# A transformer layer on one core: routed experts over token lists instead of over all tokens

## The reference

```python
h = take(weight, x)                                  # 8 x 1024 x 256
h = h + attn(layernorm(h)); h = h + ffn(layernorm(h))
# attn: L = 8 positions, N = 1024 sequences, 16 heads of 16; qkv = x @ qkv_proj.T + bias;
#       softmax(q k / 4) over the 8 positions of the same sequence; @ v; @ out_proj.T + out_bias
# ffn:  scores = sigmoid(flat @ Wg.T)                # T x 16
#       groups of 4 experts; the 2 groups with the largest sum of their top 2 stay; top 4 experts
#       topk_w = 2.5 * scores / sum(scores of the 4)
#       hid = relu(flat @ W1[e].T) ** 2              # 16 experts, 256 -> 128
#       out = sum over e of cw[t, e] * (hid @ W2[e].T)
#       shared = relu(flat @ Ws1.T) ** 2 @ Ws2.T     # 256 -> 256 -> 256
```

## Time and profile before

| | |
|---|---|
| median of three runs | 1466.54 us (1464.06 to 1471.74) |
| span of the profiled execution | 1464.6 us |
| PE, PE weight loads, DVE busy | 87%, 71%, 81% |
| ACT, POOL busy | 46%, 47% |
| DMA moved | 92.21 MB, mean 63 GB/s |

### The profile page before, as it was taken

How to read it: one execution, slowest core, us unless ns; L and a number is a source line. 1 busy time by engine, 2 the same in 40 slices (tenths; PEclk the granted TensorE clock), 3 DMA queues, 4 the chain that set the end, 5 groups by cost and what they waited for, 6 DMA issues and landing times.

```text
span 1464.6 us, 22940 instructions
## 1 busy us (share of the span) xinstructions
PE 1267.7 (87%) x7488; PEld 1033.1 (71%) x7488; DVE 1189.9 (81%) x1792; ACT 679.8 (46%) x1138; POOL 689.5 (47%) x753
## 2 busy tenths in 40 slices
PE   4458898889888899888989889898988989989898
PEld 2146767768677687767778677776867768677787
DVE  3868889697987969789797888969798797978854
ACT  2234444544444454444544444454553445445355
POOL 7744535365263635535464363536526363442600
PEclk9579999999999999999999999999999999999999
DMA  2302111111211112111111212112121111212122
GB/s 66 125 16 74 58 60 58 61 62 55 73 62 57 58 44 88 58 61 58 66 65 44 78 67 62 58 46 73 58 73 58 61 58 44 88 44 73 59 73 73
DMA packets 33748, 92.21 MB, mean 63 GB/s; under 512 B 4800, under 2 KB 13376, under 8 KB 33600
## 3 DMA queue, kind: packets, MB, share of 16 engines
q1 hardware_dynamic: 30528, 81.99, 16.7%
q0 software_dynamic: 3072, 8.39, 2.0%
HBM read 81.46 MB, written 8.91 MB: 62 GB/s over the span
## 4 chain that ended last, share of the span: by engine, by line
DVE 39%; PE 31%; issue 19%; POOL 5%; ACT 5%; DMA 1%; DVEq 1%; ACTq 0%; POOLq 0%; SPq 0%
PE psY L900 9%; PE psH L887 8%; DVE ring L684 7%; PE psB L927 5%; DVE p_sb L641 5%; DVE hid_lo L647 5%; PE psA L966 3%; DVE g_gt L723 2%; DVE ring L300 2%; PE psA L978 2%; DVE ring L302 2%; DVE ring L279 1%; DVE k_sb L666 1%; ACT hid_hi L510 1%; DVE stats L659 1%
## 5 line engine op out<-in xcount | busy, mean ns | idle before, releaser
L900 PE MATMUL psY<-w_hi,hid_hi 128*128 128x256 f32 x1152 | 339.0, 294 | 53.6 <-DVE hid_lo L647 50.3
L510 ACT CAST hid_hi<-p_sb 128x512 fp32r<-128x512 f32 x256 | 159.2, 622 | 388.8 <-DVE p_sb L641 379.5
L900 PE MATMUL psY<-w_lo,hid_hi 128*128 128x256 f32 x1152 | 330.5, 287 | 0.0
L900 PE MATMUL psY<-w_hi,hid_lo 128*128 128x256 f32 x1152 | 330.2, 287 | 0.0
L279 POOL TENSOR_TENSOR ring<-q_sb,k_sb 128x1024 f32<-128x1024 f32 x64 | 169.1, 2653 | 309.1 <-PE psA L940 205.2
L900 PEld LDWEIGHTS psY<-w_hi,hid_hi 128*128 128x128 f32 x1152 | 223.6, 194 | 107.4 <-DVE hid_lo L647 72.6
L647 DVE TENSOR_TENSOR hid_lo<-p_sb,hid_hi 128x512 fp32r<-128x512 f32 x256 | 214.6, 838 | 93.4 <-ACT hid_hi L510 73.7
L887 PE MATMUL psH<-xT_hi,w_hi 128*128 128x512 f32 x576 | 235.6, 409 | 10.9 <-issue 8.7
L641 DVE TENSOR_TENSOR p_sb<-r_sb,cwB 128x512 f32<-128x512 f32 x256 | 214.2, 837 | 34.1 <-ACT r_sb L499 27.2
L900 PEld LDWEIGHTS psY<-w_lo,hid_hi 128*128 128x128 f32 x1152 | 224.6, 195 | 9.8
L887 PE MATMUL psH<-xT_lo,w_hi 128*128 128x512 f32 x576 | 230.2, 400 | 0.0
(11 more groups left out here) (133 smaller groups left out, 2137.5 us busy)
## 6 DMA issues: line engine op xcount, KB each, us to landing
cwB<-cw_dram SPq DMA_DIRECT2D x128, 512.0 KB, 3.7
out<-h SPq DMA_DIRECT2D x32, 256.0 KB, 5.4
p_sb<-w_t SPq DMA_DIRECT2D x3, 512.0 KB
cwB<-w_t SPq DMA_DIRECT2D x3, 512.0 KB, 4.5
h<-w_t SPq DMA_DIRECT2D x2, 512.0 KB
xin<-table,idx_now POOLq DMA_INDIRECT x56
cwB<-wqkv_t SPq DMA_DIRECT2D x2, 384.0 KB, 3.2
cw_dram<-cwT SPq DMA_DIRECT2D x16, 32.0 KB, 1.6
```

The lines of the kernel that those rows point to most:

```text
L510: nc.scalar.copy(hid[0][:, e % 2, :], src[:, e % 2, :]).then_inc(hid_hi, 1)
L900: last = nc.tensor.matmul(psY[:, j // 2, (j % 2) * D:(j % 2 + 1) * D], hid[a][:, e % 2, j * P:(j + 1) * P], W2[b][:, e, :], start=(e == 0 ...
```

## The change

The kernel is rewritten in three phases, with no hardware loop; all steps are unrolled.

Phase 1 has 20 steps; step i does QKV of block i, scores and softmax of block i-1, values and output projection of block i-2, and of block i-3 the logits, the routing, the shared expert and the places of its rows. The sums over positions are now matmuls (`msum`, same form as the scores). DVE makes five of the eight products, POOL three. The values and the probabilities go to DRAM and come back in another layout (`values_io`, `probs_io`). The normalised row of a token, with its 16 weights and 16 destinations behind it (288 words), is scattered to each of the token's four experts' lists in DRAM by indirect DMA, 16 per block, the places being counted with a prefix matmul. The rows with the shared part go to `hd`.

Phase 2 runs 143 units of 256 list places. A table says for each unit its list offset and its expert; engines load these into registers. Results, multiplied by their weight, are scattered to `ys`, four rows per token. Phase 3 reads the four rows of each token and the hidden row, adds, and stores.

```diff
-    X_ALL = E + SH
+    U = 256
+    REGION = TOKENS + U
+    RW = D + 2 * E
+    UNITS = TOKENS * TOPK // U + E - 1
+    DUMMY = TOKENS * TOPK + 1
+    LAST = B + 3
...
+            def probs_io(b):            # SP
+                sp.wait_ge(probs_ready, b + 1)
+                sp.dma_start(pd[b, :].rearrange("(r t) -> r t", r=P), s_sb...).then_inc(p_stored, 16)
+                if b >= 1:
+                    sp.wait_ge(p_lo, b)
+                sp.wait_ge(p_stored, 16 * (b + 1))
+                back = pd[b, :].rearrange("(a l r n) -> a r l n", a=KH, l=L, r=64)
+                for ih in range(KH):
+                    sp.dma_start(praw[64 * ih:64 * ih + 64, :]..., back[ih]).then_inc(praw_in, 16)
...
+            for u in range(UNITS):      # SP, phase 2
+                at = sp.value_load(tab_row[0:1, 2 * u:2 * u + 1], min_val=0, max_val=E * REGION)
+                if u >= 4:
+                    sp.wait_ge(gt_mm, u - 3)
+                    sp.wait_ge(words_ready, 2 * (u - 3))
+                sp.dma_start(xg[u % 4]..., xs[bass.ds(at, U), :]...).then_inc(xg_in[u % 4], 16)
...
+            for b in range(B):          # SP, phase 3
+                if b >= 3:
+                    sp.wait_ge(out_stored[b % 3], 32 * (b // 3))
+                sp.dma_start(yk[b % 3]..., ys_v[b]).then_inc(yk_in[b % 3], 16)
+                sp.dma_start(hs[b % 3]..., hd[b]).then_inc(yk_in[b % 3], 16)
+                if b >= 2:
+                    store_out(b - 2)
...
+            def rows(b, first, count):  # POOL; called with (0, 4), (4, 4), (8, 8)
+                for c in range(first, first + count):
+                    nc.gpsimd.indirect_dma_start(xs, bass.IndirectOffsetOnAxis(pos_i[b % 2][:, c:c + 1], 0),
+                                                 xrow[b % 2][:, c // TOPK, :], None).then_inc(rows_out[b % 2], 16)
...
+            def words(u):               # POOL
+                k = u % 4
+                e = pool.value_load(tab_row[0:1, 2 * u + 1:2 * u + 2], min_val=0, max_val=E - 1)
+                pool.wait_ge(xg_in[k], 16 * (u // 4 + 1))
+                if u >= 4:
+                    pool.wait_ge(y_out[(u - 4) % 3], 16 * US * ((u - 4) // 3 + 1))
+                    pool.wait_ge(y_dve, u - 3)
+                    pool.wait_ge(y_act, u - 3)
+                nc.gpsimd.tensor_copy(yw[k][:, :], xg[k][:, :, D:D + E][:, :, bass.ds(e, 1)]...)
+                nc.gpsimd.tensor_copy(yd[k][:, :], xg[k][:, :, D + E:D + 2 * E]...[:, :, bass.ds(e, 1)]...)
+            def back(u):
+                pool.wait_ge(words_ready, 2 * (u + 1))
+                for s in range(US):
+                    pool.wait_ge(y_dve if s == 0 else y_act, u + 1)
+                    nc.gpsimd.indirect_dma_start(ys, bass.IndirectOffsetOnAxis(yd[u % 4][:, s:s + 1], 0),
+                                                 yo[u % 3][:, s, :], None).then_inc(y_out[u % 3], 16)
+            for u in range(2):
+                words(u)
+            for u in range(UNITS):
+                if u + 2 < UNITS:
+                    words(u + 2)
+                back(u)
...
+            for i in range(0, LAST + 1):    # DVE, c, a, v, r = i, i - 1, i - 2, i - 3
+                probs_lo(v); dve_product(a, 0); transposed_2_lo(r); weighted_values(v, 0)
+                dve_product(a, 1); weighted_values(v, 1); route(r, 0)
+                dve_product(a, 2); weighted_values(v, 2); route(r, 1)
+                dve_product(a, 4); weighted_values(v, 3); route(r, 2); hidden_lo(r); route(r, 3)
+                dve_product(a, 6); transposed_1_lo(c); weighted_values(v, 4); route(r, 4)
+                weighted_values(v, 5); route(r, 5); weighted_values(v, 6); add_shared(r)
+                weighted_values(v, 7); softmax_max(a); route(r, 6); route(r, 7); softmax_sum(a)
+                add_attention(v); stats_1(c + 1)
...
+            for u in range(UNITS):          # DVE, phase 2
+                if u + 2 < UNITS:
+                    up_weights(u + 2)       # value_load of the expert, copy 128x512
+                    transposed_lo(u + 2)    # 128x512 from PSUM
+                if u + 1 < UNITS:
+                    unit_lo(u + 1)          # 128x256
+                weighted(u)                 # 128x256 from PSUM
...
+            def spread(b, t):               # PE
+                g = 8 * b + t
+                if t == 0:
+                    pe.wait_ge(p_lo, b + 1)
+                if g >= 1:
+                    pe.wait_ge(av_ready, g)
+                for k, h in enumerate(PAIRS[t % 4]):
+                    last = nc.tensor.matmul(psD[:, k, :], sprd[:, h, :], pr[t // 4][:, :], start=True, stop=True)
...
+            for i in range(0, LAST + 1):    # PE
+                transpose_2(r); spread(v, 0); score(a, 0); spread(v, 1); msum(v, 0); logits(r)
+                score(a, 1); shared_up(r); spread(v, 2); msum(v, 1); score(a, 2); transpose_1(c)
+                spread(v, 3); msum(v, 2); score(a, 3); spread(v, 4); msum(v, 3); score(a, 4)
+                spread(v, 5); msum(v, 4); score(a, 5); shared_down(r); spread(v, 6); msum(v, 5)
+                score(a, 6); spread(v, 7); msum(v, 6); score(a, 7); prefix(r); msum(v, 7)
+                qkv(c, 0); rest_o(v); qkv(c, 1); out_projection(v); qkv(c, 2..5)
...
+            for u in range(UNITS):          # PE, phase 2
+                unit_transpose(u + 2)       # 4 transposes, waits for xg_in
+                unit_up(u + 1)              # 6 matmuls of 256 columns
+                unit_down(u)                # value_load of the expert, 6 matmuls of 256 columns
```

1702 lines of the change are left out of this document (998 added, 704 removed).

## The result

The changed kernel takes 1847.9 us (1845.0 to 1851.8) against 1467.5 for the kernel before: a ratio of 1.260, with an interval from 1.256 to 1.263. The forecast was 1708 us. It has the right sign but lies 140 us low: the result is outside the 1560 to 1830 that the forecast's own bounds give, and inside the full range to 1860 only because that reaches up to two rivals (half clock and landing in phase 2), neither of which is what happened. The forecast lies between the two, so both profiles are taken apart here.

A forecast was written before the change was run, and what follows sets the result against it. Three phases in a row, bound by DVE with its waits, POOL, and DMA traffic: 980 + 532 + 194 = 1706 us of span, so 1708 us measured, chance 0.54. Own bounds 1560 to 1830, full range 1470 to 1860.

The forecast's parts named there:

- half clock: Rival, phase 2: PE, busy little more than half a unit, runs at half clock; 1834 us in all, chance 0.15.
- landing: Rival, phase 2: landing of scatters paces POOL, unit 4.5 us at a landing of 5.4; 1836 us, chance 0.13.
- DVE's 44 us: Phase 1 full step: DVE's operations 41 us, plus 2.2 for one slow routing operation and 1 for waits.
- The 5 us behind PE's logits and shared layers: Phase 1 step: DVE idle 5 us because PE meets logits and shared expert layers ahead of spreads of probabilities.
- the 5.5 us: Phase 1 step head: DVE's first operation waits for probabilities to go to DRAM and back; 5.5 us stay open.
- the lower clock: Phase 1 step: PE's gaps lower its clock, 2.5 us added.
- The lower bound of 46 us: Phase 1 full step: lowest time, called DVE alone, in a range of 46 to 65 us.
- Filling and emptying (239): Phase 1 outside the 13 full steps: start 41, filling 25 and 45, emptying 50, 35 and 20, last scatters 23 us.
- POOL is the bound: Phase 2 unit: POOL's scatters 2.5, copies 0.45, register load and wait 0.6; 3.6 us, between 3.0 and 4.5.
- the forecast's own sign: Phase 2: a unit of 3.0 or over 4.3 us would mean register load or clock was judged wrongly.
- 0.6 for register load and wait: Phase 2 unit on POOL: 0.3 us each for a register load from SBUF and a wait for the copies.
- Packed streams: Rival: DVE hides the probabilities' way and PE's blocks; step 46 us, unit 3.05, total 1423 us, chance 0.15.

The follow-up runs named there:

- group 3: Four runs on a chip of their own; its unedited run of the changed kernel took 1669.5 us, the other three were edits of it.
- the run from the local buffer: Changed kernel with probabilities taken from softmax's own buffer instead of the copy returning through memory, and a quarter of the output stored: 1780.8 us.
- with one scatter: Changed kernel with one of the two scatters per phase 2 unit kept, the other block stored by a plain DMA from SP: 1638.1 us.
- the pause run: Changed kernel with a write of constants on POOL, and a wait for it, behind each scatter of phase 2: 1927.0 us.
- The fourth buffer: Changed kernel with gathers at the step's head, all products on DVE, probabilities copied ahead of the second norm, and a fourth `yo` buffer: 1624.2 us.
- group 1: Four runs of edits of the changed kernel, on a chip of their own: 1754.8, 1677.0, 1692.3 and 1780.8 us.
- the gathers-first run: Changed kernel with the four gathers of a step issued at its head, ahead of POOL's first product: 1754.8 us.
- the two products at the head: Changed kernel with gathers at the step's head, plus two DVE products ahead of the remaining probabilities and PE's head reordered: 1663.1 us.

## Why the forecast was right, and where it was not

**What bounds the kernel.** Right: three phases in a row, each with a bound of its own, cost more than the experts saved.

**Phase 1, the full step (57; 58.0 and 64.8).** DVE's 44 us were 42.1 in the stretches above; of these some 4.1 are the exclusion, where 2.2 stood, and the rest is 38 where 41 stood, so two errors hid each other. The 5 us behind PE's logits and shared layers were 5.2 + 2.0 in seven steps of group 3 (36.5 and 13.9 us), the wait at the head was 5.4, and 2.2 more went to small waits for ACT and PE. So the sum held where there are no late completions, in part by errors that cancel, and one term has a wrong name: the 5.5 us were worked out from the store and load of the probabilities, and the run from the local buffer shows that this way adds nothing to the wait. The step that failed is the sentence that DVE's first operation "waits for them": it waits for ACT, which is busy with QKV and the norm. The number, 5.5 against 5.4, agreed by luck. It is right to ask of a wait on a copy what its engine does just before. For the lower clock I had 2.5; part of each step, 17 us of 58, runs at half clock, and no run shows what that costs. The lower bound of 46 us was called DVE alone, whose sum was 44; no term makes up the rest.

**What the forecast lacked.** 6.8 us per step of late completions in the result (64.8 - 58.0), 80 us in all, and in phase 2 another 100, so 180 us between the result and group 3. With them the kernel is 26% slower, without them 14%; the forecast's 16% lies between by luck, since it knew nothing of them. No row of the kernel before could have given them: it has four gathers in a row and no late completion. The forecast did ask for the scatters' price and found it on POOL alone (1.26 us as in the earlier trace rows, which is right); who else a scatter may hold up was not asked.

**Filling and emptying (239).** In group 3 phase 1 is 68 us longer than forecast, and only 19 of them are the 13 full steps (869.5 - 109.3 = 760 against 741). The filling was right (109 us to the first L826 against 111). The emptying was not: the next two steps took 61 and 50 us where I had 50 and 35, and from the last L826 to the first transpose of a unit it was 67, where I had 43 for a step and the last scatters. I had taken from these steps the work that is missing in them; the chain through their head and tail stays, and it was what set them.

**Phase 2 (3.6; 3.66 and 2.95).** Right in length for the result, by luck, and wrong in reason. The step that failed is that POOL is the bound, with its scatters back to back; by the forecast's own sign a unit under 3.0 us, as in group 3, means that the register load or the clock was judged wrongly. In the result POOL doesn't issue back to back (its waits, 1200 to 1600 us):

```profile
POOL ys L597 <- DVE yo L1090: 107.6, 60, 3.7
```

Here is such a wait, first ACT, then POOL:

```profile
1405.37 0.47 ACT L743 ACTIVATE yo<-psO,yw 128x256 f32<-128x256 f32 x1
1408.41 0.59 ACT L724 CAST gT_hi<-psA 128x512 fp32r<-128x512 f32 x1 [2.57 <-PE psA L1337]
1411.38 0.38 ACT L730 ACTIVATE ru<-psD 128x256 f32<-128x256 f32 x1 [2.38 <-PE psD L1121]
```

```profile
1408.08 0.97 POOL L597 DMA_INDIRECT ys<-yo,yd  x1 [0.16 <-issue]
1409.36 0.96 POOL L597 DMA_INDIRECT ys<-yo,yd  x1 [0.30 <-DMA ys<-yo,yd]
1410.32 0.19 POOL L585 COPY yw<-xg 128x2 f32 x1
```

ACT has nothing for 5.5 us but one cast, while POOL issues, and goes on 1.06 us after the last scatter ended. The unit has runs of 2.0 us and then such a stop. By POOL's own pace (1404.77, 1407.61 and 1410.32 are starts of L585) a unit is 2.78 us: two scatters at 1.26 and 0.25 for the copies, which overlap. The 0.45 for the copies and 0.6 for register load and wait were too high by 0.8. In group 3 the unit is 0.17 longer than that pace. ACT and DVE wait there for a scatter to land (72 and 41 us in 250), but without these waits the unit was still 2.90, and with one scatter 2.78: what sets it stays open. Two errors cancelled: 0.8 too much on POOL, and 0.7 of late completions that I had not.

The register load was the term without a row, and I took 0.3 us for it. Its record in the pause run is 0.43 us, at least 0.29. With what follows it, it holds POOL up for 1.02 us there, where a wait stands right before it, and for less than 0.05 us in 134 of the changed kernel's 143 units, where it is ahead of its use: so the 0.3 for it didn't belong in the sum.

**Phase 3 (194; 195).** Right, with its reason: 267 GB/s at a DMA share of 0.77 in group 3 is some 350 while busy, and the bubble is 1.9 in the result and 1.6 in group 3, where I took 2.0.

**The rivals.** Packed streams: no. Half clock in phase 2: PE was 72% busy at a mean clock of 0.81 in the result, and 29 of the clock's 35 falls in phase 2 came within 3.5 us behind a late completion, so they follow the stops; without them it was 0.99 in group 3, with PE 76% busy and four transposes in each unit. Landing as pace: 0.05 us per unit at most, by the fourth buffer. Nobody had the late completions among the rivals.

## What to carry to other kernels

Indirect DMAs from GpSimd have a price on their own queue (1.26 us each here) and may have one on others: after such a change, compare the end of a matmul's record with the start of its consumer, and where they differ, try another place for some of the DMAs first; moving four gathers was worth 67 us of phase 1 on the same chip. A wait "for a copy" is a wait for whatever the copying engine does before it: find that, or a right number will stand for a wrong cause. And before filling a wait of VectorE with work, look whether GpSimd computes what ends that wait: the two can shut each other out (0.22 us became 2.37 here), and here the wait only moved. Before moving work between the two, add up what the exclusion really costs.

## What the runs showed of the hardware

- Completions of TensorE arrive up to 6.5 us behind the recorded end of the matmul while GpSimd issues indirect DMAs one after another; those of the other three engines are in time in the same traces (0.3 us at most). At the seventh product VectorE starts 1.0 to 1.9 us behind GpSimd's last gather in the result, and between 1.1 us before and 1.1 us behind it in the three other runs of group 1 that keep the gathers last, so the end of the run is not exactly what frees it. This was so on two of four chips or occasions (the result, and group 1), and on the other two in none of eight kernels, four gathers and sixteen scatters per step notwithstanding. Runs of four were enough in phase 2, while the run of eight at half clock in the gathers-first run had none. The kernel before has runs of four gathers and no late completion. Which resource it is stays open, and so does whether the chip decides it: the runs show that code alone doesn't. Whether one scatter per unit, or plain DMAs of GpSimd, would be free of it was not settled, as both ran where it doesn't occur.
- An operation of GpSimd and one of VectorE can exclude each other for their whole length: 0.22 us became 2.37 on VectorE beside a product of GpSimd, and 0.20 became 2.43 on GpSimd beside two operations of VectorE in a row. With GpSimd's products gone the 2.37 were 0.22 again, and the low halves of the probabilities took 0.71 us in the mean instead of 1.69. Which pairs of operations do this and which don't, beyond these, the runs don't show.
- The register load that GpSimd makes for a dynamic slice is recorded with 0.29 to 0.50 us in the pause run and 0.28 to 0.51 in the result. With what follows it, it costs 1.02 us where a wait stands ahead of it, and in 134 of 143 units less than 0.05 us where it doesn't.
- Four different phases 1 had a mean step of 58.0 us, and in three of them (the changed kernel in group 3, the gathers first, the two products at the head) the falls of TensorE's granted clock from 1.00 to 0.50 lie at the same places of each step in the middle of the phase, to within 0.1 us.
